# Second sweep of a graph kernel in bodies of 832 slots, with a two-operand one-hot and buffers given back by TensorE

## What is computed

```python
x_l = (h @ W_l + b_l).reshape(n, H, F); x_r = (h @ W_r + b_r).reshape(n, H, F)
m = leaky_relu(x_l[src] + x_r[dst] + e_emb, 0.2)
alpha = einsum('ehf,hf->eh', m, att)
ex = exp(alpha - segment_max(alpha, dst)[dst])
out = segment_sum(x_l[src] * (ex / denom[dst])[..., None], dst).mean(axis=1) + bias
# batch norm, relu, residual; then the second layer:
mean_aggr = segment_sum(h2[src], dst) / max(deg, 1)
x = x + mean_aggr @ w_l.T + h2 @ w_r.T + b
```

## Time and profile before

| | us |
|---|---|
| median of 3 runs | 6262.49 |
| lowest, highest | 6259.12, 6267.76 |
| profiled execution | 6257.39 |
| its span in the trace | 6256.1 |

### The profile page before, as it was taken

One profiled execution on the slowest core, in us unless ns is written; L12 is line 12 of the kernel. 1 busy time (PEld: TensorE's weight loads), 2 busy tenths in 40 slices (PEclk: granted clock), 3 DMA queues, 4 the chain that ended last, 5 costly groups with the idle time before them and its releaser, 6 DMA issues. The chain is left out here.

```text
span 6256.1 us, 80221 instructions
## 1 busy us (share of the span) xinstructions
PE 4144.8 (66%) x16664; PEld 3019.4 (48%) x16665; DVE 3615.2 (58%) x9117; ACT 1150.2 (18%) x4355; POOL 3831.8 (61%) x3799
## 2 busy tenths in 40 slices
PE   2888888888888864888888886713433433333337
PEld 1666666666666652444444443613333333333336
DVE  6666666666666668888888889862222222222224
ACT  1111111111111112444444442210000000000001
POOL 2577777777777743444444441437777777777770
PEclk8999999999999986999999999655555555555555
DMA  7344444444444431333323331111111111111111
GB/s 104 105 130 131 126 134 130 133 127 132 131 132 128 132 84 58 84 86 86 84 86 86 86 86 37 36 42 26 26 26 26 26 26 26 26 26 26 26 26 24
DMA packets 633247, 478.12 MB, mean 76 GB/s; under 512 B 452024, under 2 KB 460344, under 8 KB 632812
## 3 DMA queue, kind: packets, MB, share of 16 engines
q1 hardware_dynamic: 468218, 258.72, 16.3%
q0 software_dynamic: 104800, 108.55, 9.3%
q10 hardware_dynamic: 60050, 109.22, 4.7%
HBM read 350.04 MB, written 126.05 MB: 76 GB/s over the span
## 5 line engine op out<-in xcount | busy, mean ns | idle before, releaser
L512 POOL DMA_INDIRECT ZR<-hD,mS x1664 | 1592.3, 957 | 612.6 <-issue 489.9
L1117 POOL DMA_INDIRECT BIG<-h2D,mS x1564 | 1481.6, 947 | 573.8 <-issue 472.4
L1138 PE MATMUL PS<-BIG,ZR 128*128 x3328 | 814.5, 428 | 1267.6 <-DMA BIG<-h2D,mS 1252.6
L1138 PEld LDWEIGHTS PS<-BIG,ZR 128*128 128x128 f32 x3328 | 740.1, 328 | 1342.3 <-DMA BIG<-h2D,mS 1326.3
L807 PE MATMUL PS<-R,ZR 128*128 128x329 f32 x3328 | 1152.1, 496 | 196.9 <-DVE ZR L741 177.4
L1152 DVE TENSOR_TENSOR BIG<-BIG,PS 128x64 f32 x1664 | 364.7, 219 | 1409.6 <-PE PS L1138 1367.9
L542 PE MATMUL PS<-Wz,R 128*128 128x264 f32 x3328 | 1060.2, 401 | 80.0 <-issue 78.1
L570 DVE SCALAR_TENSOR_TENSOR PS<-PS,a 128x528 f32<-128x528 f32 x832 | 596.2, 717 | 810.1 <-PE PS L543 802.9
L791 POOL TENSOR_TENSOR R<-ZR,R 128x768 f32<-128x768 f32 x416 | 615.6, 1480 | 716.7 <-ACT R L777 684.2
L543 PE MATMUL PS<-BIG,R 128*128 x3328 | 1033.7, 393 | 0.0
L807 PEld LDWEIGHTS PS<-R,ZR 128*128 128x128 f32 x3328 | 578.9, 201 | 769.8 <-DVE ZR L741 505.6
(11 more groups left out here) (212 smaller groups left out, 2405.7 us busy)
## 6 DMA issues: line engine op xcount, KB each, us to landing
zD<-ZR ACTq DMA_DIRECT2D x416, 256.0 KB, 2.1
ZR<-zD SPq DMA_DIRECT2D x416, 256.0 KB, 2.6
R<-relD SPq DMA_DIRECT2D x105, 512.0 KB
ZR<-ea SPq DMA_DIRECT2D x1664, 32.0 KB
ZR<-hD,mS POOLq DMA_INDIRECT x1664, 2.4
BIG<-h2D,mS POOLq DMA_INDIRECT x1564, 2.4
AL<-hD SPq DMA_DIRECT2D x28, 224.0 KB, 2.8
lmS<-lmD SPq DMA_DIRECT2D x106, 32.0 KB, 2.2
```

What stands on the lines that cost most here:

```text
L512: Q.indirect_dma_start(zring[:, j % 32, 0, :], None, hD, bass.IndirectOffsetOnAxis(mS[:, j // 16, j % 16:j % 16 + 1], 0)).then_inc(hs[q], 16)
L1117: Q.indirect_dma_start(ACC[:, j % NB, j // NB * F:j // NB * F + F], None, h2D, bass.IndirectOffsetOnAxis(mS[:, (j // 16) % 4, j % 16:j % 1 ...
L1138: P.matmul(PS[:, j % 7, 0:F], oh[:, (j // 4) % 4, j % 4, :], rows, start=True, stop=True).then_inc(a3_rdy.s, 1)
```

## The change

It makes the bodies of the second sweep 832 slots long, so that each loop runs twice instead of 26 times; all sizes and indices follow `L2`. The lists `BANK2` and `TAKE2` go: the bank is the slot's number modulo 7, each slot takes one token, the three taken ahead of the loop go, and the tokens start at 5 instead of 6. The one-hot of a slot is a `tensor_tensor` of `iota_ps` and the slot's column of `mR` broadcast to 128 columns, instead of a `tensor_scalar` with that column as a per-partition scalar. And `hbf`, which lets SyncE load the next stored rows into a buffer, is given by TensorE once it has `x_rdy` and `px_rdy` of a quad, instead of by VectorE every fourth slot.

```diff
@@ -731,41 +731,41 @@
     barrier()
 
     v(V.tensor_copy(iota_ps, iota))
-    BANK2 = [j % 7 for j in range(63)] + [3]
-    TAKE2 = [0, 0, 0, 4, 0, 0, 0] + [1] * 56 + [4]
+    L2 = NS // 2
 
     def rows2(q):
         return R[:, 4 * (q % 4):4 * (q % 4) + 4, :]
 
     def onehot2(s):
-        return V.tensor_scalar(oh[:, (s // 4) % 4, s % 4, :], iota_ps, mR[:, (s // 16) % 4, s % 16:s % 16 + 1], None, ALU.is_equal)
+        return V.tensor_tensor(oh[:, (s // 4) % 4, s % 4, :], iota_ps,
+                               bc(mR[:, (s // 16) % 4, s % 16:s % 16 + 1], [128, 128]), ALU.is_equal)
 
     mr[0].take(V, 16)
     for s in range(12):
         k = onehot2(s)
-    k.then_inc(o2_rdy.s, 6)
+    k.then_inc(o2_rdy.s, 5)
     close(mr[0])
 
     def load_quads():
 
-        with S.Fori(0, NS // 64) as i:
-            for q in range(16):
+        with S.Fori(0, NS // L2) as i:
+            for q in range(L2 // 4):
                 half, k = q // 4, q % 4
                 if k == 1:
                     mrf.take(S)
-                    load_rel(ds(i * 4 + half + 2, 1), (half + 2) % 4)
-                    load_maxima((i * 4 + half + 2) * 64, (half + 2) % 4)
+                    load_rel(ds(i * (L2 // 16) + half + 2, 1), (half + 2) % 4)
+                    load_maxima((i * (L2 // 16) + half + 2) * 64, (half + 2) % 4)
                 hbf.take(S)
                 S.dma_start(hb[:, k, :, :, :].rearrange("p s t f -> p (s t f)"),
-                            zD[ds(i * 16 + q, 1), :, :].rearrange("a p c -> (a p) c")).then_inc(hq[k].s, 16)
+                            zD[ds(i * (L2 // 4) + q, 1), :, :].rearrange("a p c -> (a p) c")).then_inc(hq[k].s, 16)
             close(mrf, hbf)
 
     def last_head():
 
-        with A.Fori(0, NS // 64) as i:
-            for q in range(16):
+        with A.Fori(0, NS // L2) as i:
+            for q in range(L2 // 4):
                 k = q % 4
-                alq4 = ahead(A, AL[:, ds(i * 256 + 16 * q, 16)].rearrange("p (s h) -> p s h", h=4))
+                alq4 = ahead(A, AL[:, ds(i * (4 * L2) + 16 * q, 16)].rearrange("p (s h) -> p s h", h=4))
                 rbf.take(A)
                 r = rows2(q)
                 A.copy(r[:, :, 256:260], alq4).then_inc(hx.s, 1)
@@ -783,8 +783,8 @@
 
     def first_heads():
 
-        with Q.Fori(0, NS // 64):
-            for q in range(16):
+        with Q.Fori(0, NS // L2):
+            for q in range(L2 // 4):
                 hx.take(Q)
                 hz.take(Q)
                 r = rows2(q)
@@ -795,34 +795,31 @@
 
     def sums2():
 
-        o2_rdy.take(P, 3)
-        close(o2_rdy)
-        with P.Fori(0, NS // 64):
-            for j in range(64):
+        with P.Fori(0, NS // L2):
+            for j in range(L2):
                 if j % 4 == 0:
                     x_rdy.take(P)
                     px_rdy.take(P)
-                if TAKE2[j]:
-                    o2_rdy.take(P, TAKE2[j])
-                P.matmul(PS[:, BANK2[j], 0:AC], oh[:, (j // 4) % 4, j % 4, :], rows2(j // 4)[:, j % 4, :],
+                    P.sem_inc(hbf.s, 1)
+                o2_rdy.take(P)
+                P.matmul(PS[:, j % 7, 0:AC], oh[:, (j // 4) % 4, j % 4, :], rows2(j // 4)[:, j % 4, :],
                          start=True, stop=True).then_inc(ag_rdy.s, 1)
             close(x_rdy, px_rdy, o2_rdy)
 
     def adds2():
 
-        with V.Fori(0, NS // 64) as i:
-            vt = Table(V, bT, i, "wb", NB - 1, 64)
-            for j in range(64):
+        with V.Fori(0, NS // L2) as i:
+            vt = Table(V, bT, i, "wb", NB - 1, L2)
+            for j in range(L2):
                 a, s = ahead(V, BIG[:, ds(vt(j) * AC, AC)]), j + 12
                 ag_rdy.take(V)
                 if j % 4 == 3:
                     V.sem_inc(rbf.s, 1)
-                    V.sem_inc(hbf.s, 1)
                 c2_acc.take(V)
-                V.tensor_tensor(a, a, PS[:, BANK2[j], 0:AC], ALU.add).then_inc(c2_acc.s, 1)
+                V.tensor_tensor(a, a, PS[:, j % 7, 0:AC], ALU.add).then_inc(c2_acc.s, 1)
                 if s % 16 == 0:
                     mr[(s // 16) % 4].take(V, 16)
-                onehot2(s % 64).then_inc(o2_rdy.s, 1)
+                onehot2(s % L2).then_inc(o2_rdy.s, 1)
                 if j % 16 == 15:
                     V.sem_inc(mrf.s, 1)
             close(ag_rdy, c2_acc, *mr)
```

## The result

The changed kernel takes 6033.1 us (median of 4 runs, 6011.1 to 6037.2) where the kernel before took 6260.8 in the same set of runs: a ratio of 0.963, 95% interval 0.960 to 0.966. That is 228 us less, 227 were forecast. Beside the last set of experiments it gave 0.963 again (0.961 to 0.964).

A forecast was written before the change was run, and what follows sets the result against it. VectorE bounds the second sweep. Fewer body ends (138 us) and a cheaper one-hot (90 us), hbf worth 0, make the sweep 1105 us, 227 less: 6262.5 - 227 = 6035 us, range 6005 to 6100.

The forecast's parts named there:

- What bounds the sweep: Second sweep: VectorE never waits within slots, 0.665 us each; register loads and 5.75 us at each body's end add to it.
- The one-hot: VectorE's comparison in each slot: two operands cut its pitch from 0.26 to 0.20 us, the slot to 0.603, 90 us less.
- the 512-column relative: L468 in the third sweep, same comparison with both inputs broadcast, 0.68 us long; scaled down to 0.285 us for 128 columns.
- the tier table: Skill's DVE perf modes: tensor_scalar may run in a higher mode than tensor_tensor; read as against the edit, undecisive at 128 columns.
- The hole: VectorE's gap at the register load every 16 slots: stays 2.07 us from add 14 to add 16.
- The seams: Ends of loop bodies in the second sweep: 25 become 1, 138 us less; the one left costs 7 us, bounds 5.75 and 12.
- Streaming: Queues fetching straight-line code in the long bodies: taken as 0; rival of stalls at each 8 KB, 6399 us, chance 0.04.
- The sign I named: What would show in the new sweep's profile: more instruction packets in q14, with no hole at their times.
- The total of 1105 us: New second sweep: 104 groups of 10.51 us make 1093, plus 5 for first filling and 7 for the remaining body end.
- TensorE's lead and clock: Second sweep: waiting one slot later stays hidden, 0.554 us a slot under 0.603, 8% to spare; clock stays at 2.4 GHz.
- hbf worth 0, bounds 0 and -5: Stored-row buffers released by TensorE some eight slots earlier: the old order would just hold, so no gain, at most 5 us.
- VectorE's lost record in four slots: Moving the hbf signal takes one record per four slots off VectorE's queue, adds one to TensorE's; hidden, queues run ahead.
- the page's size of 512 instructions: Skill's held code per engine other than TensorE: a 64-slot body would not be fetched again; packets and gap speak against it.

The follow-up runs named there:

- the last set of experiments: Changed kernel with 32 block numbers per register load instead of 16: 6019.0 us; also with one 1664-slot body: 6018.8; the changed kernel again beside them: 6028.1.

## Why the prediction was right, point by point, and where it wasn't

**What bounds the sweep** was right: start-to-start pitches of VectorE, with a hole at each register load and a seam at each branch. Predicted for the new sweep 1105 us, measured 1105.3.

**The one-hot** was right: 0.603 us a slot predicted, 0.604 measured; 0.285 us long predicted, 0.284 measured. The scaling from the 512-column relative carried it. By an estimate from the formula of the Trainium skill (VectorE: DVE Perf Modes, the section on the TRN2 errata) it would have been 290 ns. The prediction took the tier table of the same page to speak against the edit. It doesn't: the page goes on to say, under Why PSUM operands drop a tier, that fp32 from PSUM runs at one element a cycle, and that holds for either form. Why the scalar form takes 61 ns more isn't shown.

**The hole** was right: 2.07 us from add 14 to add 16 predicted, 0.604 + 1.451 = 2.055 measured, so only 14 of 16 pitches shrank.

**The seams** were right in size: the last one took 5.82 us, 7 were allowed. The gap behind the branch is 3.2 us (2998.1 to 3001.3), where it was 3.5, so VectorE paid no more for its jump when the four other queues jumped far back beside it.

**Streaming** was costed at nothing and is not quite free. Over the median pitches the slots lose 7.5 us in all: 4.3 in the twelve late adds of VectorE's own stops, 0.36 in the one for which TensorE came late, the rest in slots late by a tenth of a us or less. My expectations for the long bodies alone and for hbf by VectorE still put this down as 0.36 us each 256 queue records, which misread the step at 2519.80 and an average distance. The sign I named was wrong too: there are fewer packets of q14 in the sweep than before, 110 against 128, and 28 of 16 KB on q8 where there was one. The q8 packets are TensorE's, not VectorE's. In this sweep they mostly stand 255 of TensorE's records apart, there are 28 also with hbf by VectorE, where VectorE has some 420 records more, and VectorE's fetches at the seams of the kernel before moved none of them.

The total of 1105 us came out to within 1 us by luck. The seam took 5.82 - 1.45 = 4.4 us beyond the hole that stands there anyway (7 allowed), the first three slots lost 1.1 + 1.1 + 1.2 - 3 x 0.6 = 1.6 us (5 allowed), and the streaming took 7.5 (0 allowed): small errors that cancelled.

**TensorE's lead and clock** were right: a matmul half is 441 ns long at the median and the clock is 1.00 through 540 us on end. This is the row of the windows view for 2450 to 2990, columns as in the earlier trace rows:

```profile
2450.00:2990.00 540.00, 505.45 (x1638) 245.51 (x1637) 498.67 (x1632) 322.32 (x1426) 301.92 (x204) 1.00 0.37 104
```

**hbf worth 0, bounds 0 and -5** was right only inside the whole change, where it is 4 us of sweep as far as two chips can tell, and wrong as a statement on the part. Alone it is worth 117 us. The step that failed is the sentence that VectorE's lost record in four slots is hidden because queues run ahead of their engines. I had read the seam as a fetch of code, with the body's length as its cause, but did not ask how near to the bound the body was, nor that another part of the change shortens it. The long bodies and hbf remove the same 3.5 us at the same seams: 142 + 68 + 117 = 327 us alone, 228 together. So the sum was right and the names on its terms were right for one order of applying them only. Given hbf and the one-hot, the long bodies bring 14 to 18 us.

The Trainium skill (Runtime: NRT & Kernel Launch, Instruction fetch mechanics) describes both effects: a branch to a page outside the two that are held stalls, and code comes in blocks of 256 instructions (16 KB) whose bound is mostly hidden. The runs agree with both and give the prices, 3.2 to 3.5 us for the branch and 0.35 us for a bound that shows. For VectorE they show packets of 8 KB, each 128 records, and not of 16; for TensorE of 16. The prediction held the packets of a 292-record body against the page's size of 512 instructions. They don't contradict it: two blocks of 256 that meet at record 32 of the body, and end at record 288, would hold a body of 284 records and not one of 292.

**What stays open.** By the traces the bound of this loop is its record 288, because the loop begins where it does against the grid of 128 records. That a body of the same length is held or fetched according to where it begins is worked out, not shown: no run moved a body without changing it. Nor is it shown how many of the 8 KB pieces VectorE holds, three or four.

## What to carry to other kernels

Count the queue records of each engine's loop body before anything else is done to a loop with idle "issue" at its seams, and look at the gap behind the branch and at the instruction packets. Where the body begins against the grid of packets may count beside its length. A body just over the bound can be cured by moving one semaphore signal to another engine, while doubling its length may make it worse. When two parts of a change remove the same wait, cost them in both orders; the total may be right while the credit is not. And cost small VectorE operations by start-to-start pitch, scaled from a relative with the same operands in the same memories.

## What the runs showed of the hardware

- VectorE's loop: 276 and 284 queue records in a body run from held code (0.3 us behind the branch, three packets in the sweep), as are 248; 292 are fetched again at each turn (3.5 us, 128 packets). This loop's 8 KB packets belong to its records 32, 160 and 288.
- In straight line VectorE's code comes in 8 KB packets, one each 128 queue records. The queue stops for about 0.35 us at a bound; 12 of some 54 bounds in the changed sweep made an add late. TensorE's comes in 16 KB packets on q8, 255 records apart, 28 in the sweep, and made one add late, by 0.36 us.
- A register load takes 1.11 us for 16 numbers and 2.11 for 32.
- A comparison of 128 columns in PSUM is 61 ns shorter, in length and in pitch, with the per-partition value as a broadcast operand than as a scalar.
